# Normalising batch 1 of x from a transposed load, with the context work re-ordered around it

## The chip, the cores and the metric

The kernel runs on one core of one Trainium2 chip. The metric is the device time of one execution in microseconds (us). TensorE is called PE below, VectorE DVE, ScalarE ACT, GpSimd POOL and SyncE SP.

## What is computed

One decoder layer on x of shape (2, 512, 1024): self-attention with a head width of 256, a product of quantised activations with a quantised context, and a sparse feed-forward part, each on a layer norm of x and added to it. Cut to what matters here:

```python
def _L0_attn_ref(x, Wqkv, bqkv, Wo, bo):
    qkv = jnp.einsum('bsc,cf->bsf', x, Wqkv) + bqkv          # q, k, v: 256 wide each
    attn = jax.nn.softmax(jnp.einsum('bqd,bkd->bqk', q, k) * scale, axis=-1)
    out = jnp.einsum('bqk,bkd->bqd', attn, v)
    return jnp.einsum('bqd,dc->bqc', out, Wo) + bo

def _L0_xattn_ref(x1, x2, ...):                              # x2 is ctx_4096
    return jnp.matmul(fake_quant(x1, ...), fake_quant(x2, ...))

x = x + _L0_attn_ref(_layernorm(x), Wqkv, bqkv, Wo, bo)
x = x + _L0_xattn_ref(_layernorm(x), ctx_4096, ...)
x = x + _L0_ffn_ref(_layernorm(x), c1_w, c2_w, w1, w2t)
```

## The kernel before

x lies in SBUF as 8 tiles of 128 tokens by 1024 features; tiles 0 to 3 are batch 0, tiles 4 to 7 batch 1. PE needs the features on partitions. So each tile is normed by ACT (`norm`), transposed by PE in 8 blocks of 128x128 (`transpose_norm`, two jobs "T1" of four blocks for a tile), and cut into a high part (`hi_T` on ACT) and a low part (`lo_T` on DVE). Every product in the attention is then three matmuls, high by high, high by low, low by high (`split_mm`). The weights are cut in the same way, the high part on ACT and the low part on POOL.

All five engines run an order written out by hand, and wait on counting semaphores. PE writes its results into a ring of six PSUM banks. `job_order` lists the jobs in PE's order, and `take_bank` makes a job wait until the job six places ahead of it has been read out, which the counter `bank_free` says. DVE frees the banks, in its own program order, so a bank that DVE frees late holds up a PE job even when the data would be there.

The jobs of the first 110 us are: "T1" (transposes of normed x), "V" (values, 48 matmuls of 256 columns each), "Q" with c = 0 to 3 (queries and keys, 24 matmuls of 512 columns each), "S" (scores, four jobs of 6), "PT" (transposes of the softmax, four jobs of 4 blocks), "O" (values mixed by the softmax, two jobs of 12), "WO" (output projection, 6 each). The first number of a job is its batch.

Beside this, sixteen context tiles of 128x1024 are quantised. SP loads tile i into one of four slots (`ctx_slot`; slots 0 and 1 show as `ctx_raw` in the trace, slots 2 and 3 as `xn`), and the load of tile i waits until tile i-4 has left its slot (`q2_done`). ACT scales it (`scale_ctx`), DVE clips and rounds it (`round_ctx`), and POOL casts it to bf16 into `q2` (line 530). POOL also adds up the eight tiles of a batch (`add_q2`, line 515), adds the output bias to x (line 504) and cuts the low part of Wo (`cut_Wo`, line 521), which the first "WO" job waits for. Tiles 8 to 15 go to the place of the q and k weights, so tile 8 waits for job Q(1,3). Wo is loaded by ACT's queue at line 889, behind `hi_V(1, 1)`, into a place that the low part of x held.

The feed-forward part, from about 185 us to the end, is loops in which PE is never idle for long.

Of the kernel before, what the change touches and what calls it, by code (L numbers as in the profile page):

```python
# [98 lines left out]
def decoder_layer(nc, x_in, ctx_in, wqkv, bqk, bv, wo, bo, s1, z1, s2, z2, c1, c2, w1, w2, out):  # L99
# [35 lines left out]

    W_hi = at("W_hi", 96, [P, 3, KD, HD], F32R)
# [91 lines left out]
    with ExitStack() as ctx:  # L228
# [16 lines left out]
        W_loaded = [[sem(f"W_loaded{i}_{h}") for h in range(2)] for i in range(3)]  # L245
        bias_loaded = sem("bias_loaded")
# [28 lines left out]
        normed = sem("normed")  # L275
        vbias_added = sem("vbias_added")
# [127 lines left out]
        def _(sp):  # L404
# [81 lines left out]
        def _(pool):  # L486
# [15 lines left out]
            for t in range(NT):  # L502
                pool.wait_ge(normed, t + 1)
                nc.gpsimd.tensor_tensor(x[:, t, :], x[:, t, :], bo_b[:, :], ALU.add).then_inc(bo_added, 1)
# [32 lines left out]
            cut_Wo()  # L537
# [134 lines left out]
        def _(act):  # L672
# [40 lines left out]

            def hi_W(i, h):
# [4 lines left out]
            def hi_Q(b, c):  # L719
# [3 lines left out]
                if b == 1 and c == 0:  # L723
                    act.wait_ge(W_lo_done, 6)
# [134 lines left out]

            roots(0, 4)  # L860
            norm(0, 4)
            norm(0, 5)
            hi_Q(0, 0)
            hi_Q(0, 1)
            both(hi_T, 0, 4)
            norm(0, 6)
            hi_Q(0, 2)
            both(hi_T, 0, 5)
            norm(0, 7)
            hi_Q(0, 3)  # L870
            both(hi_T, 0, 6)
            both(hi_T, 0, 7)
# [3 lines left out]
            act.wait_ge(qp_ready, 1)  # L876
            for i in range(4):
                scale_ctx(i)
# [137 lines left out]
        def _(dve):  # L1016
# [56 lines left out]

            def lo_Q(b, c):
# [234 lines left out]
            lo_Q(0, 0)  # L1309
            lo_Q(0, 1)  # L1310
            lo_T(0, 4)
            lo_Q(0, 2)
            lo_T(0, 5)
            lo_Q(0, 3)
            lo_T(0, 6)
            lo_T(0, 7)

# [8 lines left out]
            nc.vector.scalar_tensor_tensor(rb_add, rb_mul, float(D), d1, ALU.mult, ALU.mult).then_inc(qp_ready, 1)  # L1326
            maxima(0)
# [4 lines left out]
            for i in range(4):  # L1332
                round_ctx(i)
# [139 lines left out]
        def _(pe):  # L1473
# [19 lines left out]
            def transpose_norm(rnd, t):  # L1493
# [4 lines left out]
                for h in range(2):  # L1498
# [6 lines left out]
                    last.then_inc(mm_done, 1)  # L1505

# [278 lines left out]
            project_qk(0, 0)  # L1785
            project_qk(0, 1)
            transpose_norm(0, 4)
            project_qk(0, 2)
            transpose_norm(0, 5)
            project_qk(0, 3)  # L1790
            transpose_norm(0, 6)
            transpose_norm(0, 7)
            for i in range(TB):
                scores(0, i)
            made("T1", NT - 1, 1)
            for c in range(4):
                project_qk(1, c)
            project_v(1, 0)
# [104 lines left out]
```

## Time and profile before

| | us |
|---|---|
| three executions | 793.71, 793.86, 794.48 |
| median | 793.86 |
| the profiled execution | 794.16 |
| its span in the trace | 792.3 |

The trace is of one execution. Its span is 1.9 us shorter than its own time, and its own time is 0.3 us over the median. PE's granted clock is full (1.00, which is 2.4 GHz) in every stretch of the trace.

### The profile page before, as it was taken

The page shows a single profiled execution, that of the slowest core. Times are in us where ns is not written, and L with a number is a line of the kernel's source. Part 1 is how long each engine was busy: PE and PEld are TensorE (multiplying, and loading weights), DVE is VectorE, ACT ScalarE, POOL GpSimd, SP SyncE. Part 2 cuts the span into 40 slices and gives each one's busy share as a digit, 9 for nine tenths or more (in the row PEclk, how much of TensorE's full clock was granted, in tenths as well). Part 3 has the DMA queues.
Part 4 walks back from the last instruction along what each step waited for, and adds up shares of the span by engine and source line. Part 5 has one row for each costly group of instructions (what it writes and reads, how often), then busy time and mean ns, then how long its engine had stood idle before and what let it go on. Part 6 is the DMA issues. An engine that isn't in the chain of part 4 may idle for free.

```text
span 792.3 us, 11474 instructions
## 1 busy us (share of the span) xinstructions
PE 785.7 (99%) x3883; PEld 641.2 (81%) x3888; DVE 590.7 (75%) x962; ACT 249.7 (32%) x375; POOL 433.2 (55%) x265
## 2 busy tenths in 40 slices
PE   8999999999999999999999999999999999999998
PEld 8888987478888888888888888888888888888886
DVE  6655669887884878887877778787878787777864
ACT  6457666973321130312121221303031212212030
POOL 3935898576999954545445252535454543525240
PEclk9999999999999999999999999999999999999999
DMA  9126402000111110111111111111111121111104
GB/s 340 66 106 212 164 19 89 8 1 8 60 54 60 37 49 29 54 60 53 60 53 60 53 60 53 58 34 37 43 53 60 53 60 53 60 53 53 53 18 195
DMA packets 22615, 53.22 MB, mean 67 GB/s; under 512 B 4544, under 2 KB 6592, under 8 KB 22464
## 3 DMA queue, kind: packets, MB, share of 16 engines
q1 hardware_dynamic: 22448, 51.86, 18.9%
q10 hardware_dynamic: 144, 1.05, 0.4%
q8 instruction: 15, 0.25, 0.1%
q14 instruction: 8, 0.07, 0.0%
HBM read 48.70 MB, written 4.19 MB: 67 GB/s over the span
## 4 chain that ended last, share of the span: by engine, by line
PE 96%; DVE 2%; DMA 1%; issue 0%; ACT 0%; SPq 0%; DVEq 0%
PE bank L1770 13%; PE bank L1771 13%; PE bank L1772 13%; PE bank L1675 12%; PE bank L1677 11%; PE bank L1676 11%; PE bank L1488 4%; PE bank L1490 4%; PE bank L1489 4%; PE bank L1629 3%; PE bank L1684 2%; PE bank L1666 2%; DMA x<-x_in 1%; PE bank L1645 1%; PE bank L1504 1%; DVE xT_lo L1070 1%
## 5 line engine op out<-in xcount | busy, mean ns | idle before, releaser
L1770 PE MATMUL bank<-w_hi,h_hi 128*128 128x512 f32 x448 | 176.2, 393 | 0.0
L1771 PE MATMUL bank<-w_lo,h_hi 128*128 128x512 f32 x448 | 175.0, 391 | 0.0
L1772 PE MATMUL bank<-w_hi,h_lo 128*128 128x512 f32 x448 | 174.4, 389 | 0.0
L1277 DVE TENSOR_TENSOR x<-bank,x 128x512 f32<-128x512 f32 x208 | 133.5, 685 | 50.0 <-PE bank L1772 50.0
L564 POOL TENSOR_TENSOR lo_r<-r,slot 128x512 fp32r<-128x512 f32 x52 | 67.5, 1299 | 155.9 <-ACT slot L787 155.9
L1772 PEld LDWEIGHTS bank<-w_hi,h_lo 128*128 128x128 f32 x448 | 84.1, 188 | 18.0
L1770 PEld LDWEIGHTS bank<-w_hi,h_hi 128*128 128x128 f32 x448 | 84.1, 188 | 15.7
L1771 PEld LDWEIGHTS bank<-w_lo,h_hi 128*128 128x128 f32 x448 | 84.4, 188 | 15.2
L1675 PE MATMUL bank<-xT_hi,slot 128*128 128x512 f32 x240 | 95.0, 396 | 0.0
L1676 PE MATMUL bank<-xT_lo,slot 128*128 128x512 f32 x240 | 93.5, 390 | 0.0
L1677 PE MATMUL bank<-xT_hi,lo_r 128*128 128x512 f32 x192 | 74.8, 390 | 0.0
L569 POOL TENSOR_TENSOR w_lo<-w_raw,w_hi 128x1024 fp32r<-128x1024 f32 x28 | 69.4, 2479 | 9.3 <-ACT w_hi L803 9.3
L830 ACT ACTIVATE h_hi<-bank 128x512 fp32r<-128x512 f32 x56 | 33.3, 599 | 127.3 <-DVE bank L1222 103.6
L649 POOL TENSOR_TENSOR tmp<-r,r 128x512 f32<-128x512 f32 x12 | 15.5, 1291 | 102.1 <-DMA r<-w 102.1
L787 ACT ACTIVATE slot<-r 128x512 fp32r<-128x512 f32 x66 | 41.3, 629 | 77.9 <-DMA r<-w 44.1
L814 ACT ACTIVATE sums<-bank 128x512 f32<-128x512 f32 x12 | 7.2, 598 | 171.5 <-PE bank L1677 171.5
L1218 DVE SCALAR_TENSOR_TENSOR h_lo<-bank,h_hi 128x512 fp32r<-128x512 f32 x56 | 38.4, 691 | 26.8 <-ACT h_hi L830 26.2
L1675 PE MATMUL bank<-T_hi,slot 128*128 128x512 f32 x144 | 57.3, 398 | 0.0
L1676 PE MATMUL bank<-T_lo,slot 128*128 128x512 f32 x144 | 56.0, 389 | 0.0
L1222 DVE TENSOR_TENSOR bank<-bank,sums 128x512 f32<-128x512 f32 x48 | 33.6, 700 | 26.7 <-PE bank L1684 25.8
L1676 PEld LDWEIGHTS bank<-xT_lo,slot 128*128 128x128 f32 x240 | 45.1, 188 | 8.8
L1675 PEld LDWEIGHTS bank<-xT_hi,slot 128*128 128x128 f32 x240 | 45.1, 188 | 8.8
(205 smaller groups left out, 1599.5 us busy)
## 6 DMA issues: line engine op xcount, KB each, us to landing
r<-w SPq DMA_DIRECT2D x56, 256.0 KB, 3.5
w_raw<-w SPq DMA_DIRECT2D x28, 512.0 KB, 4.0
x<-x_in SPq DMA_DIRECT2D x8, 512.0 KB, 10.0
ctx_raw<-ctx_in SPq DMA_DIRECT2D x8, 512.0 KB, 3.5
xn<-ctx_in SPq DMA_DIRECT2D x8, 512.0 KB, 4.8
out<-x SPq DMA_DIRECT2D x7, 512.0 KB, 2.7
W_raw<-wqkv SPq DMA_DIRECT2D x6, 512.0 KB, 10.5
c_raw<-c SPq DMA_DIRECT2D x112, 16.0 KB, 2.0
```

What stands on the lines that cost most here:

```text
L564: nc.gpsimd.tensor_tensor(lo[:, :, :], raw[:, :, :], hi[:, :, :].bitcast(F32), ALU.subtract).then_inc(A_lo_done, 1)
L569: nc.gpsimd.tensor_tensor(w2_lo[:, j, :], w2_raw[:, j, :], w2_hi[:, j, :].bitcast(F32), ALU.subtract).then_inc(w2_lo_done, 1)
L787: nc.scalar.activation(slot[:, :, :], src[:, :, :], ACT.Copy).then_inc(A_hi_done, 1)
L1218: nc.vector.scalar_tensor_tensor(h_lo[:, r, s], bank[c_bank(g, r, b)][:, :], 0.0, h_hi[:, r, s].bitcast(F32), ALU.max, ALU.subtract).then_ ...
L1222: return nc.vector.tensor_tensor(dst, bank[src][:, :], part, ALU.add).then_inc(sum_done, 1)
L1277: nc.vector.tensor_tensor(x[:, t, c], bank[unit_banks(g)[p]][:, :], x[:, t, c], ALU.add).then_inc(unit_added, 1)
L1675: nc.tensor.matmul(dst, hi[:, k, :], B_hi[:, k, :], start=first and k == 0, stop=False)
L1676: nc.tensor.matmul(dst, hi[:, k, :], B_lo[:, k, :], start=False, stop=False)
L1677: last = nc.tensor.matmul(dst, lo[:, k, :], B_hi[:, k, :], start=False, stop=closed and k == H - 1)
L1770: nc.tensor.matmul(dst, h_hi[:, j, m], w2_hi[:, j, c], start=j == 0, stop=False)
L1771: nc.tensor.matmul(dst, h_hi[:, j, m], w2_lo[:, j, c], start=False, stop=False)
L1772: last = nc.tensor.matmul(dst, h_lo[:, j, m], w2_hi[:, j, c], start=False, stop=j == GJ - 1)
```

## The change

The host passes a second copy of batch 1 of x with the features on partitions (`xT_in`). SP loads it in one DMA of 2 MB behind the last tile of x, into `xT_raw`, which lies where the low part of transposed batch 1 goes.

Batch 1 is then normed there. PE spreads the row scales and shifts of a pair of tiles over all partitions, by four 128x128 transposes of a broadcast column (`spread_rows`, job "R"). DVE multiplies and adds in place (`norm_xT`, two halves of 128x1024 each, a multiply and an add for each), ACT takes the high part (`hi_xT`), POOL the low part (`lo_xT`, in the place of `lo_T` on DVE). The transposes of tiles 4 to 7, the four ACT norms and the eight `hi_T` and `lo_T` of these tiles are gone. The bias additions of tiles 4 to 7 no longer wait for the norm.

The job V(1,0) moves ahead of the scores of batch 0. Context loads start behind Q(0,3). Context tiles 0 to 3 are scaled and rounded ahead of the softmax of batch 0, around V(1,0). Tiles 13, 14 and 15 each move one place back on ACT and DVE; tile 15's rounding now stands behind the maxima of batch 1 and ahead of `inverse_sums(1)`. On POOL the low part of Wo is cut ahead of tile 15 in place of behind the sum `add_q2(0, 5)`, and two sums no longer wait for the rounding of tile 8.

The core of the diff (a mechanical change of line numbers and of the counter for `normed` is left out):

```diff
-    jobs = both("T1", 0) + both("T1", 1) + both("T1", 2) + [("V", 0, 0)] + both("T1", 3) + [("V", 0, 1)]
-    jobs += [("Q", 0, 0), ("Q", 0, 1)] + both("T1", 4) + [("Q", 0, 2)] + both("T1", 5)
-    jobs += [("Q", 0, 3)] + both("T1", 6) + both("T1", 7)
+    jobs = both("T1", 0) + both("T1", 1) + both("T1", 2) + [("V", 0, 0)] + both("T1", 3)
+    jobs += [("V", 0, 1), ("Q", 0, 0), ("R", 0), ("Q", 0, 1), ("R", 1), ("Q", 0, 2), ("Q", 0, 3), ("V", 1, 0)]
     jobs += [("S", 0, i) for i in range(4)]
-    jobs += [("Q", 1, c) for c in range(4)] + both("V", 1)
+    jobs += [("Q", 1, c) for c in range(4)] + [("V", 1, 1)]
...
+            sp.dma_start(xT_raw[:, :, :], xT_in).then_inc(xT_loaded, 16)
-            sp.wait_ge(mm_done, nth("T1", 7, 1) + 1)
+            sp.wait_ge(mm_done, nth("Q", 0, 3) + 1)
...
+            def lo_xT(p):
+                for h in range(2):
+                    pool.wait_ge(xT_hi_done, 2 * p + h + 1)
+                    at_pair = token_pair(p, h)
+                    nc.gpsimd.tensor_tensor(xT_lo[1][at_pair], xT_raw[at_pair], xT_hi[1][at_pair].bitcast(F32),
+                                            ALU.subtract).then_inc(xT_lo_done, 1)
+            add_bo(0, 1, 2, 3)
+            lo_xT(0)
+            add_bo(4)
+            lo_xT(1)
+            add_bo(5, 6, 7)
...
+            def hi_xT(p):
+                for h in range(2):
+                    if h == 0:
+                        act.wait_ge(xT_normed, p + 1)
+                    else:
+                        act.wait_ge(bank_free, nth("R", p) + 1)
+                    at_pair = token_pair(p, h)
+                    nc.scalar.activation(xT_hi[1][at_pair], xT_raw[at_pair], ACT.Copy).then_inc(xT_hi_done, 1)
...
+            def norm_xT(p):
+                dve.wait_ge(mm_done, nth("R", p) + 1)
+                dve.wait_ge(xT_loaded, 16)
+                row = job_bank("R", p)[:, :].rearrange("p (s o m) -> p s o m", s=2, o=1)
+                scale, shift = (row[:, s].to_broadcast([P, 4, 2 * P]) for s in range(2))
+                for h in range(2):
+                    part = xT_raw[token_pair(p, h)]
+                    link(nc.vector.tensor_tensor(part, part, scale, ALU.mult))
+                    last = nc.vector.tensor_tensor(part, part, shift, ALU.add)
+                    if h == 0:
+                        last.then_inc(xT_normed, 1)
+                free(last)
...
+            def spread_rows(p):
+                pe.wait_ge(rstd_ready, nth_chain(0, TB) + 1)
+                take_bank("R", p)
+                for s, rows in enumerate((rstd, nmr)):
+                    for i in range(2):
+                        t, c = TB + 2 * p + i, (2 * s + i) * P
+                        last = nc.tensor.transpose(job_bank("R", p)[:, c:c + P],
+                                                   rows[:, t:t + 1].to_broadcast([P, P]), id_f[:, :])
+                last.then_inc(mm_done, 1)
```

On PE, around the job Q(0,2). `bank` is the PSUM ring, `id_f` the identity, and the matmuls of `xT` and `W` are those of the projection. Before:

```order
L1490 MATMUL bank<-xT_hi_50,W_lo 128x512
L1504 MATMUL bank<-id_f,xn 128x128 [waits bank_free,normed]
L1504 MATMUL bank<-id_f,xn 128x128 x3
L1504 MATMUL bank<-id_f,xn 128x128 [waits bank_free]
L1504 MATMUL bank<-id_f,xn 128x128 x3
L1488 MATMUL bank<-xT_hi_50,W_hi 128x512 [waits W_lo_done,bank_free]
```

And now, behind Q(0,0), where `rstd` and `nmr` are the scales and shifts:

```order
L1534 MATMUL bank<-xT_hi_50,W_lo 128x512
L1558 MATMUL bank<-id_f,rstd 128x128 [waits bank_free,rstd_ready]
L1558 MATMUL bank<-id_f,rstd 128x128
L1558 MATMUL bank<-id_f,nmr 128x128 x2
L1532 MATMUL bank<-xT_hi_50,W_hi 128x512 [waits W_lo_done,bank_free]
```

Eight transposes for each of four tiles have become four for each of two pairs, and they stand one projection earlier.

On POOL, from context tile 8 (`q_1`) to the end of the sums of batch 0 (`q_sum`). Before:

```order
L530 TENSOR_SCALAR q_1_73<-ctx_raw 128x1024 [waits mm_done]
L530 TENSOR_SCALAR q_1_73<-ctx_raw 128x1024 [waits ctx_rounded]
L530 TENSOR_SCALAR q_1_73<-xn 128x1024 [waits ctx_rounded] x2
L515 TENSOR_TENSOR q_sum_83<-q_sum_83,q_0_72 128x1024 [waits summing]
L530 TENSOR_SCALAR q_1_73<-ctx_raw 128x1024 [waits ctx_rounded] x2
L515 TENSOR_TENSOR q_sum_83<-q_sum_83,q_0_72 128x1024 [waits summing]
L530 TENSOR_SCALAR q_1_73<-xn 128x1024 [waits ctx_rounded] x2
L515 TENSOR_TENSOR q_sum_83<-q_sum_83,q_0_72 128x1024 [waits summing]
L521 TENSOR_TENSOR Wo_lo<-Wo_raw,Wo_hi 128x2048 [waits Wo_hi_done]
L515 TENSOR_TENSOR q_sum_83<-q_sum_83,q_0_72 128x1024 [waits summing] x2
```

Now:

```order
L558 TENSOR_SCALAR q_1_74<-ctx_raw 128x1024 [waits ctx_rounded,mm_done]
L558 TENSOR_SCALAR q_1_74<-ctx_raw 128x1024 [waits ctx_rounded]
L558 TENSOR_SCALAR q_1_74<-xn 128x1024 [waits ctx_rounded] x2
L541 TENSOR_TENSOR q_sum_84<-q_sum_84,q_0_73 128x1024 [waits summing]
L558 TENSOR_SCALAR q_1_74<-ctx_raw 128x1024 [waits ctx_rounded] x2
L541 TENSOR_TENSOR q_sum_84<-q_sum_84,q_0_73 128x1024 [waits summing]
L558 TENSOR_SCALAR q_1_74<-xn 128x1024 [waits ctx_rounded]
L547 TENSOR_TENSOR Wo_lo<-Wo_raw,Wo_hi 128x2048 [waits Wo_hi_done]
L558 TENSOR_SCALAR q_1_74<-xn 128x1024 [waits ctx_rounded]
L541 TENSOR_TENSOR q_sum_84<-q_sum_84,q_0_73 128x1024 [waits summing] x3
```

The cut of Wo has moved ahead of the cast of tile 15 and of one sum.

On DVE, from the rounding of tile 12 to the maxima of batch 1 there are, now:

```order
L1187 TENSOR_SCALAR ctx_raw<-ctx_raw 128x1024 [waits ctx_scaled]
L1138 TENSOR_TENSOR bank<-bank,bv_b 128x512 [waits mm_done]
L1142 TENSOR_TENSOR v_lo_69<-bank,v_hi_67 128x512 [waits hi_done]
L1162 TENSOR_TENSOR pT_lo<-bank,pT_hi 128x4x128 [waits hi_done] x2
L1187 TENSOR_SCALAR ctx_raw<-ctx_raw 128x1024 [waits ctx_scaled]
L1162 TENSOR_TENSOR pT_lo<-bank,pT_hi 128x4x128 [waits hi_done] x2
L1187 TENSOR_SCALAR xn<-xn 128x1024 [waits ctx_scaled]
L1392 TENSOR_SCALAR ones_r<-id_f 128x128
```

and behind the maxima, where before the reciprocals (`pinv`, which free the banks of the scores) came at once:

```order
L1150 TENSOR_SCALAR nbias<-smax 128x1 [waits vec]
L1187 TENSOR_SCALAR xn<-xn 128x1024 [waits ctx_scaled]
L1157 RECIPROCAL pinv<-psum_row 128x1 [waits exp_done] x4
L1168 TENSOR_TENSOR oT_lo_79<-bank,oT_hi_77 128x512 [waits hi_done] x2
L1162 TENSOR_TENSOR pT_lo<-bank,pT_hi 128x4x128 [waits hi_done] x4
```

The rounding of tile 15 (`xn<-xn`) now stands between the maxima and the reciprocals.

## Rows read from the trace of the kernel before

**Rows 1.** Page: busy time by engine; then who PE waited for, longest first.
```profile
PE 785.7 (99%) x3883; PEld 641.2 (81%) x3888; DVE 590.7 (75%) x962; ACT 249.7 (32%) x375; POOL 433.2 (55%) x265
PE bank L1645 <- DVE xT_lo L1070: 0.6, 1, 0.6
```

**Rows 2.** Timeline of PE: start us, us, engine, line, op, out<-in, count.
```profile
32.33 0.39 PE L1488 MATMUL bank<-xT_hi,W_hi 128*128 128x512 f32 x1
...
37.77 1.03 PE L1504 MATMUL bank<-id_f,xn 128*128 128x128 f32 x8
38.56 0.48 PE L1488 MATMUL bank<-xT_hi,W_hi 128*128 128x512 f32 x1
38.88 0.40 PE L1489 MATMUL bank<-xT_lo,W_hi 128*128 128x512 f32 x1
39.11 0.39 PE L1490 MATMUL bank<-xT_hi,W_lo 128*128 128x512 f32 x1
...
50.47 1.91 PE L1504 MATMUL bank<-id_f,xn 128*128 128x128 f32 x16
52.29 0.47 PE L1488 MATMUL bank<-k_hi,q_hi 128*128 128x512 f32 x1
```

**Rows 3.** Timeline of DVE: the last step of the norm statistics, and two low parts.
```profile
32.18 0.13 DVE L1062 SCALAR_TENSOR_TENSOR nmr<-mv,bank 128x4 f32<-128x4 f32 x1
...
39.36 1.28 DVE L1070 TENSOR_TENSOR xT_lo<-bank,xT_hi 128x512 fp32r<-128x512 f32 x2
```

**Rows 4.** Timeline of PE, later: V(1,0), PT(0), PT(1) and WO(0,0) start.
```profile
79.59 0.28 PE L1488 MATMUL bank<-W_hi,xT_hi 128*128 128x256 f32 x1
...
91.11 1.91 PE L1576 MATMUL bank<-id_f,probs 128*128 128x128 f32 x16
...
103.77 1.91 PE L1576 MATMUL bank<-id_f,probs 128*128 128x128 f32 x16
...
105.43 0.49 PE L1488 MATMUL bank<-Wo_hi,oT_hi 128*128 128x512 f32 x1
```

**Rows 5.** Timelines of DVE and POOL: two roundings and the POOL work beside them.
```profile
62.03 1.24 DVE L1142 TENSOR_SCALAR ctx_raw<-ctx_raw 128x1024 f32<-128x1024 f32 x1 [0.44 <-ACT ctx_raw L763]
77.34 2.35 DVE L1142 TENSOR_SCALAR ctx_raw<-ctx_raw 128x1024 f32<-128x1024 f32 x1 [0.44 <-ACT ctx_raw L763]
...
61.69 1.04 POOL L530 TENSOR_SCALAR q<-ctx_raw 128x1024 bf16<-128x1024 f32 x1 [12.12 <-DVE ctx_raw L1142]
...
76.99 2.15 POOL L515 TENSOR_TENSOR q_sum<-q 128x1024 fp32r<-128x1024 bf16 x1 [1.36 <-DVE ctx_raw L1142]
```

**Rows 6.** View of the tile `ctx_raw` from 83.0 to 84.5 us: tile 12's load.
```profile
DMA to landing us min/median/max: 3.5/3.5/3.5
```

**Rows 7.** Timeline of ACT: tile 12, high part of V(1,1), Wo, softmax transposes.
```profile
86.79 1.25 ACT L763 ACTIVATE ctx_raw<-ctx_raw,qp,qd 128x1024 f32<-128x1024 f32 x1
...
92.04 0.60 ACT L736 ACTIVATE v_hi<-bank 128x512 fp32r<-128x512 f32 x1 [1.57 <-DVE bank L1093]
...
92.54 1.08 ACT L752 ACTIVATE pT_hi<-bank 128x512 fp32r<-128x512 f32 x2
...
96.86 1.93 ACT L897 ACTIVATE Wo_hi<-Wo_raw 128x2048 fp32r<-128x2048 f32 x1
```

**Rows 8.** Timeline of DVE: V(1,1), tile 15, two maxima of batch 1.
```profile
91.31 0.70 DVE L1093 TENSOR_TENSOR bank<-bank,bv_b 128x512 f32<-128x512 f32 x1
...
96.88 0.69 DVE L1142 TENSOR_SCALAR xn<-xn 128x1024 f32<-128x1024 f32 x1 [0.21 <-ACT xn L763]
...
97.62 0.69 DVE L1104 TENSOR_REDUCE smax<-bank 128x1 f32<-128x512 f32 x1
...
98.41 0.68 DVE L1104 TENSOR_REDUCE smax<-bank 128x1 f32<-128x512 f32 x1
```

**Rows 9.** Timeline of POOL: the cut of Wo, and the first corrections of x.
```profile
100.77 4.60 POOL L521 TENSOR_TENSOR Wo_lo<-Wo_raw,Wo_hi 128x2048 fp32r<-128x2048 f32 x1
...
131.72 10.13 POOL L551 TENSOR_TENSOR x<-x,corr 128x1024 f32<-128x1024 f32 x4 [3.35 <-ACT xn L704]
```

More of the change, by code:

```diff
@@ L96, in nth_chain, with decoder_layer @@
     return next(n for n, (r, first, count) in enumerate(CHAINS) if r == rnd and first <= t < first + count)
-def decoder_layer(nc, x_in, ctx_in, wqkv, bqk, bv, wo, bo, s1, z1, s2, z2, c1, c2, w1, w2, out):
+def decoder_layer(nc, x_in, xT_in, ctx_in, wqkv, bqk, bv, wo, bo, s1, z1, s2, z2, c1, c2, w1, w2, out):
     D = x_in.shape[2]
@@ L275, in decoder_layer @@
         normed = sem("normed")
+        xT_normed = sem("xT_normed")
+        xT_hi_done = sem("xT_hi_done")
+        xT_lo_done = sem("xT_lo_done")
         vbias_added = sem("vbias_added")
@@ L501, in _, with add_bo @@
             pool.wait_ge(bias_loaded, 48)
-            for t in range(NT):
-                pool.wait_ge(normed, t + 1)
-                nc.gpsimd.tensor_tensor(x[:, t, :], x[:, t, :], bo_b[:, :], ALU.add).then_inc(bo_added, 1)
+            def add_bo(*tiles):
+                for t in tiles:
+                    if t < TB:
+                        pool.wait_ge(normed, t + 1)
+                    else:
+                        pool.wait_ge(mv_done, t + 1)
+                    nc.gpsimd.tensor_tensor(x[:, t, :], x[:, t, :], bo_b[:, :], ALU.add).then_inc(bo_added, 1)
+            def lo_xT(p):
[9 more added lines that the diff above has]
+            add_bo(5, 6, 7)
             def add_q2(b, i):
@@ L730, in hi_V @@
                 act.wait_ge(vbias_added, 2 * b + i + 1)
+                if (b, i) == (1, 0):
+                    act.wait_ge(W_lo_done, 6)
                 if (b, i) == (0, 0):
@@ L860, in _ @@
             roots(0, 4)
-            norm(0, 4)
-            norm(0, 5)
             hi_Q(0, 0)
             hi_Q(0, 1)
-            both(hi_T, 0, 4)
-            norm(0, 6)
+            hi_xT(0)
             hi_Q(0, 2)
-            both(hi_T, 0, 5)
-            norm(0, 7)
+            hi_xT(1)
             hi_Q(0, 3)
-            both(hi_T, 0, 6)
-            both(hi_T, 0, 7)
+            act.wait_ge(qp_ready, 1)
+            scale_ctx(0)
+            scale_ctx(1)
+            hi_V(1, 0)
+            scale_ctx(2)
+            scale_ctx(3)
             for i in range(TB):
                 exp(0, i)
-            act.wait_ge(qp_ready, 1)
-            for i in range(4):
-                scale_ctx(i)
             for c in range(4):
@@ L1309, in _ @@
             lo_Q(0, 0)
+            norm_xT(0)
             lo_Q(0, 1)
-            lo_T(0, 4)
+            norm_xT(1)
             lo_Q(0, 2)
[L1313 to L1316, printed above, removed]
             dve.wait_ge(qp_loaded, 64)
@@ L1326, in _ @@
             nc.vector.scalar_tensor_tensor(rb_add, rb_mul, float(D), d1, ALU.mult, ALU.mult).then_inc(qp_ready, 1)
+            lo_Q(0, 3)
+            round_ctx(0)
+            round_ctx(1)
+            lo_V(1, 0)
+            round_ctx(2)
+            round_ctx(3)
             maxima(0)
@@ L1330, in _ @@
             nc.vector.tensor_copy(id_b[:, :], id_f[:, :]).then_inc(id_b_ready, 1)
-            for i in range(4):
-                round_ctx(i)
             for c in range(4):
@@ L1785, in _ @@
             project_qk(0, 0)
+            spread_rows(0)
             project_qk(0, 1)
-            transpose_norm(0, 4)
+            spread_rows(1)
             project_qk(0, 2)
-            transpose_norm(0, 5)
             project_qk(0, 3)
-            transpose_norm(0, 6)
-            transpose_norm(0, 7)
+            pe.wait_ge(xT_lo_done, 2)
+            project_v(1, 0)
             for i in range(TB):
                 scores(0, i)
-            made("T1", NT - 1, 1)
+            pe.wait_ge(xT_lo_done, 4)
             for c in range(4):
                 project_qk(1, c)
-            project_v(1, 0)
             project_v(1, 1)
```

31 lines of the change are left out of this document (17 added, 14 removed).

## The prediction, as it was put on record

> **What bounds the kernel now.** I read the page first: PE is busy for 99% of the span, and the waits of PE add up to little (the longest behind the start is 0.6 us, on DVE at line 1645) [rows 1]. So PE's own work is the time, and a change pays only by what it takes off PE. Next I read PE's timeline where the transposes of batch 1 stand, to price them [rows 2], and then, since the change also turns the order on ACT, DVE and POOL, the stretch from 80 to 106 us on each of them [rows 4 to 9]. What the reader should see there: the cut of Wo on POOL ends at 105.37 [rows 9], and the first output projection, which needs it, starts at 105.43 [rows 4]. PE does not wait there now, but it has less than 0.1 us in hand. Anything that brings PE there earlier gains only if POOL and DVE come earlier too.
>
> **What PE loses and gets.** The transposes of tile 4 hold PE from 37.77 to 38.56, 0.79 us, and the first matmul behind them takes 0.32 us to the next where 0.23 is usual: 0.88 in all [rows 2]. Tile 5 is like it: 0.9. The 16 transposes of tiles 6 and 7 take 50.47 to 52.29, with the same 0.09 behind: 1.9. Together 3.7 us for 32 transposes. The change adds 8 such transposes in two pieces, at 0.11 each: 0.9 us. Net on PE: 2.8 us less.
>
> **The new wait at the first piece.** `spread_rows(0)` needs the shifts `nmr`, which end at 32.18 + 0.13 = 32.31 [rows 3]. PE comes there at 32.33 [rows 2]. With about 0.1 us from DVE to PE, that costs 0.1 us. Matmuls of Q(0,1) queue behind it.
>
> **The norm on DVE, ACT and POOL: hidden.** No row shows a 128x1024 operation with one operand in PSUM of this form. The nearest is the pair of 128x512 subtractions from a bank, 1.28 us [rows 3], so 1.2 us for each of four operations, 4.8 us for a pair of tiles; at double that it would be 9.6. DVE starts pair 0 behind `lo_Q(0, 0)` at about 34, and frees R(0) at 39. ACT's two copies end near 41 and POOL's two subtractions (2.4 us each, half of the cut of Wo [rows 9]) near 45. V(1,0) needs them at 49.7. So there is 4.7 us of cover, and it would hold even at 1.9 us for each operation. Pair 1 is needed only 11 us later, at the projections. What leaves these engines (four norms, eight copies, eight subtractions) is worth nothing, as they were hidden. The 2 MB load has to land by 34. It is the size of four loads like that of tile 12 (3.5 us each [rows 6]), so it takes up to 14 us behind the last tile of x, and it is issued behind all of x and W. I put it at nothing; rival 4 has the other end.
>
> **PE up to the softmax of batch 0.** On the clock of the trace, V(1,0) takes 5.76 us (half of 79.59 to 91.11 [rows 4]). It moves from behind Q(1,3) to ahead of the scores. So Q(1,3), which ended at 79.59, ends at 79.59 - 2.8 + 0.1 + 5.76 = 82.7. V(1,1) ends at 88.4, the four PT jobs at 90.1 (1.66 us [rows 4]).
>
> This is the step that matters. **Tiles 8 to 15 start on POOL only behind Q(1,3), now 3.1 us later, while all that waits for POOL is due 2.7 us earlier.**
>
> **POOL and DVE do not run these operations side by side.** A rounding on DVE takes 0.69 us by itself (96.88 [rows 8]). The one at 62.03 took 1.24 and ended at 63.27; POOL's cast beside it ended at 62.73. The one at 77.34 took 2.35 and ended at 79.69; POOL's sum beside it ended at 79.14 [rows 5]. Both end 0.55 us behind the end of POOL's instruction: the rounding waits for POOL and then runs. The subtractions from a bank (1.28 for two at 39.36 [rows 3]) ran beside POOL's bias additions at their usual length.
>
> The Trainium skill ("SBUF — State Buffer", "SBUF: two separate sides") says that DVE in a two-port mode and GpSimd share a port pair that is locked for a whole instruction, the later one blocking fully. By that rule, the trace agrees, a rounding behind the 4.6 us cut of Wo waits for all of it, and this speaks against putting them side by side, as the change does.
>
> **The chain behind Q(1,3), step by step.** Cast 1.04 [rows 5], sum 2.15 [rows 5], scale 1.24 [rows 7], about 0.2 from PE's last matmul to another engine (91.11 to 91.31 [rows 4, 8]) and 0.05 to 0.1 between other engines.
>
> - Casts of tiles 8 and 9: 82.9 to 85.0. ACT has scaled tile 10 by 84.75 (high part of Q(1,3) 0.6, scale 1.24), its rounding meets cast 9 and ends at 85.5; cast 10 ends at 86.6; the rounding of tile 11 meets it, ends at 87.2; cast 11 ends at 88.3. The sum `add_q2(0, 3)` follows, to 90.4.
> - Tile 12 loads when cast 8 is over, 83.9, and takes 3.5 us [rows 6]: scaled by 88.7, its rounding comes 0.4 to 0.5 us behind the start of that sum and ends at 91.0. DVE does the bias of V(1,1) only then, to 91.6 (now at once, at 91.31 for a job that ended at 91.11), ACT the high part to 92.2, DVE the low part to 92.9. The job S(1,1) stands six behind V(1,1), and PE comes there at 90.1 + 0.1 + 1.37 = 91.6. It gets the bank at 93.0. **First stall: 1.45 us.**
> - ACT: two softmax copies (1.0), scale of tile 13, 94.3. Rounding 95.0, cast 96.1, sum `add_q2(0, 4)` to 98.3. ACT has two more copies and tile 14 by 96.45; the rounding meets the sum and ends at 98.85. Cast 14 to 99.95, then the cut of Wo to 104.5 (4.6 us [rows 9]). The high part of Wo comes 4.8 us behind that of V(1,1) and takes 1.9 [rows 7], so it is over by 98.9 and does not hold the cut.
> - DVE: four maxima at 0.79 [rows 8] from 98.9, to 102.1. Then the rounding of tile 15 meets the cut of Wo and ends at 105.1. Behind it are the reciprocals that free the score banks. PE comes to PT(1,0), which needs the first of them, at 93.0 + 3 x 1.37 + 5.45 = 102.6, and starts at 105.3. **Second stall: 2.7 us.** PT(1) takes 1.66 and the first output projection starts at 106.95. The low part of Wo is there by then, and so are the two low parts of O, 1.3 us behind the reciprocals. The exponentials (tile 15 now stands ahead of them on ACT) end at about 103 and don't decide.
>
> Put through the same steps the kernel before gives 105.55 for that start, where the trace has 105.43. So the difference is 106.95 - 105.55 = 1.4 us later. By terms: -2.8 + 0.1 + 1.45 + 2.7 = +1.45.
>
> **Behind that point** PE has no wait up to 171 us, and the order is unchanged. POOL ends its sums some 2.8 us later than now, 1.4 later against PE; ahead of the corrections of x it is idle for 3.35 us, until ACT's norm [rows 9], and that takes it up. So 1.4 us stays to the end. The profiled execution of 794.16 would be 795.6; with the median at 793.86, 795.3.
>
> **Rivals.**
>
> 1. *The rounding of tile 12 comes ahead of the sum.* It takes a load of at most 3.0 us in place of 3.5, or POOL 0.5 us later. Then the bias of V(1,1) is done 1.5 us earlier, the first stall is gone and the chain behind ends 2.1 us earlier; the second stall stays, at about 2.0 (PE 2.7 us early, held to 103.2). -2.8 + 0.1 + 2.0 = -0.7: 793.1. For it: the margin is half a microsecond. Against: the load's own row says 3.5.
> 2. *The roundings don't wait for POOL where PE depends on them*, because DVE gets in first, or the long cut does not lock it out. Then the first output projection waits only for the cut of Wo, some 0.8 us: -2.7 + 0.8 = -1.9, and with a better course of POOL -2.7: 791.2 to 792.0. Against it speak both rows of the pair above.
> 3. *Slower by more.* The mechanism: behind the second stall PE's granted clock falls from 2.4 to 1.2 GHz. The trace shows full clock throughout, and the longest wait in it behind the start is 0.6 us [rows 1], so it can't say. If only the four PT jobs ran at half the clock, 1.66 would become 3.3: 1.7 us more, 797.0. It decides from the point where the two stalls pass 4.3 us in sum (over 0.2% slower then even without it); I have 4.15.
> 4. *The load of x transposed delays the first 25 us.* It would need to be served ahead of x or W; it is issued last. Price: up to the 14 us above. I give it 3 in 100, which are part of rival 3's share.
>
> In the Trainium skill ("TensorE: Matmul & The Clock Gate", "HAM oscillation — how this bites in real kernels") idle waits between bursts are said to bring the clock back down; no run here shows it. By that rule the time would be that of rival 3.
>
> **Chances and range.** What I forecast 60 in 100 (794.8 to 795.8, as the steps are good to a few tenths), rival 1 15, rival 2 11, rival 3 with 4 14. This kernel's measurement can tell some 0.2% from no change, 1.6 us. Faster by that (under 792.3): rival 2, 0.12. Slower by that (over 795.4): rivals 3 and 4 and a third of my case, 0.33. Within: 0.55. The range takes in my case, rival 1 and the near part of rival 3: 792.8 to 796.8.
>
> **What would show it.** In the new trace: PE without the 32 transposes and with 8 (right if PE reaches V(1,0) at about 49.7 without a wait); the rounding of tile 12 at about 88.8 with some 2.1 us; a wait of PE on `v_lo` ahead of S(1,1); the rounding of tile 15 at about 102 with 3 us, ending 0.55 behind the cut of Wo; PT(1) at 105.3. It is wrong if the roundings keep 0.7 us beside POOL, or if PE waits for `xT_lo` at V(1,0) or at Q(1,0).

## The result, and the profile after

The changed kernel takes 797.71 us (median of 6 runs, 797.41 to 798.09), the kernel before 793.98 (6 runs, 793.70 to 794.48). The ratio is 1.0046, 95% interval 1.0033 to 1.0059: slower by 3.7 us. The forecast was 795.3, and the result lies above the range, whose end was 796.8.

The profiled execution of the changed kernel, by its page: busy time by engine, and the granted clock in 40 slices. Beside [rows 1], PE's busy time is 0.6 us less, for 3.7 us more of span.

```profile
span 796.0 us, 11421 instructions
PE 785.1 (99%) x3859; PEld 639.4 (80%) x3864; DVE 611.7 (77%) x962; ACT 245.5 (31%) x367; POOL 442.0 (56%) x269
...
PEclk9999999999999999999999999999999999999999
```

Who PE waited for (total us, times, longest). The first and the third are new: before, the longest wait behind the start was 0.6 [rows 1].

```profile
PE bank L1631 <- DVE pinv L1157: 2.4, 1, 2.4
PE bank L1834 <- POOL id_f L498: 1.5, 1, 1.5
PE bank L1532 <- DVE v_lo L1142: 1.3, 1, 1.3
PE bank L1700 <- DVE xT_lo L1101: 0.6, 1, 0.6
...
PE bank L1671 <- ACT q1T L806: 0.2, 1, 0.2
```

PE's timeline (start us, us, engine, line, operation, idle before it and who ended it): the first piece of broadcast, R(0), in its two parts, then the starts of V(1,0), PT(0), S(1,1), PT(1) and WO(0,0). They answer to [rows 2, 4].

```profile
32.62 0.43 PE L1558 MATMUL bank<-id_f,rstd 128*128 128x128 f32 x2
32.89 0.38 PE L1558 MATMUL bank<-id_f,nmr 128*128 128x128 f32 x2
...
49.94 0.28 PE L1532 MATMUL bank<-W_hi,xT_hi 128*128 128x256 f32 x1
...
88.67 1.91 PE L1631 MATMUL bank<-id_f,probs 128*128 128x128 f32 x16
93.26 0.50 PE L1532 MATMUL bank<-k_hi,q_hi 128*128 128x512 f32 x1 [1.29 <-DVE v_lo L1142]
...
105.45 3.43 PE L1631 MATMUL bank<-id_f,probs 128*128 128x128 f32 x16 [2.37 <-DVE pinv L1157]
108.53 0.77 PE L1532 MATMUL bank<-Wo_hi,oT_hi 128*128 128x512 f32 x1
```

The 16 transposes of PT(1) hold PE for 108.53 - 105.45 = 3.08 us, where before they held it for 1.66. The windows of 1 us say why. Columns: stretch; its length; busy us and counts of PE, PE's weight loads, DVE, ACT, POOL; then the granted clock, the share of the DMA engines and GB/s.

```profile
104.00:105.00 1.00, 0.00 (x0) 0.00 (x0) 1.00 (x1) 0.18 (x1) 0.77 (x1) 1.00 0.00 0
105.00:106.00 1.00, 0.55 (x4) 0.56 (x5) 1.00 (x6) 0.00 (x0) 0.59 (x1) 0.88 0.00 0
106.00:107.00 1.00, 1.00 (x7) 1.00 (x6) 0.78 (x3) 0.60 (x1) 1.00 (x2) 0.50 0.00 0
107.00:108.00 1.00, 1.00 (x6) 1.00 (x5) 0.84 (x2) 0.60 (x1) 1.00 (x1) 0.50 0.00 0
108.00:109.00 1.00, 1.00 (x6) 1.00 (x5) 0.84 (x2) 0.69 (x2) 0.92 (x2) 0.50 0.07 16
109.00:110.00 1.00, 1.00 (x5) 0.78 (x5) 0.84 (x2) 0.98 (x2) 1.00 (x1) 0.92 0.00 0
```

Behind the wait of 2.37 us PE works at half the clock, 1.2 GHz, from about 105.8 to 109.2 us (windows of 0.2 us place the two ends). That is 3.4 us, in which 1.7 us of work at full clock get done. The page's 40 slices don't show it: a slice is 20 us long, and 3.4 us of it at half the clock round away.

Timelines of DVE and of POOL around the two waits: the roundings of tiles 12 and 15, and what POOL did beside them.

```profile
89.90 1.34 DVE L1187 TENSOR_SCALAR ctx_raw<-ctx_raw 128x1024 f32<-128x1024 f32 x1 [2.44 <-ACT ctx_raw L799]
91.16 0.68 DVE L1138 TENSOR_TENSOR bank<-bank,bv_b 128x512 f32<-128x512 f32 x1
...
102.31 3.02 DVE L1187 TENSOR_SCALAR xn<-xn 128x1024 f32<-128x1024 f32 x1
105.24 0.33 DVE L1157 RECIPROCAL pinv<-psum_row 128x1 f32<-128x1 f32 x4
```

```profile
88.55 2.14 POOL L541 TENSOR_TENSOR q_sum<-q_sum,q 128x1024 fp32r<-128x1024 f32 x1
...
100.20 4.57 POOL L547 TENSOR_TENSOR Wo_lo<-Wo_raw,Wo_hi 128x2048 fp32r<-128x2048 f32 x1
105.41 1.05 POOL L558 TENSOR_SCALAR q<-xn 128x1024 bf16<-128x1024 f32 x1 [0.64 <-DVE xn L1187]
```

The cut of Wo ends at 104.77, the rounding at 105.33, 0.56 us behind it; the rounding of tile 12 ends at 91.24, 0.55 behind the sum (90.69).

**Where the 3.7 us are**, by PE's start times in both traces: PT(0) at 88.67 instead of 91.11, so -2.44. From PT(0) to PT(1) 16.78 us instead of 12.66: +4.12, the two waits with PE's restarts. PT(1) +1.42 and the rest of the half clock +0.28, together 1.70. That leaves PE 3.38 later than before at the start of O(1,0) (114.38 against 111.00). The first matmul behind the last transposes of x, ahead of the feed-forward part, starts 3.76 later than before (175.47 against 171.71), so another 0.38 was lost in between. -2.44 + 4.12 + 1.70 + 0.38 = 3.76.

### The profile page after: what moved, and what is told of

Read it like the earlier page. It is cut to its first block, busy times and chain, and to the rows that moved or that the text cites. A ratio compares the mean times of both kernels' runs of the same rounds, so it can differ in the third digit from the quotient of the medians.

```text
span 796.0 us, 11421 instructions
## 1 busy us (share of the span) xinstructions
PE 785.1 (99%) x3859; PEld 639.4 (80%) x3864; DVE 611.7 (77%) x962; ACT 245.5 (31%) x367; POOL 442.0 (56%) x269
## 3 DMA queue, kind: packets, MB, share of 16 engines
q1 hardware_dynamic: 22592, 53.96, 19.6%
## 4 chain that ended last, share of the span: by engine, by line
PE 90%; DVE 4%; ACT 2%; DMA 2%; issue 1%; POOL 0%; SPq 0%; ACTq 0%; DVEq 0%
PE bank L1825 13%; PE bank L1826 13%; PE bank L1827 13%; PE bank L1730 12%; PE bank L1732 11%; PE bank L1731 11%; PE bank L1532 3%; PE bank L1534 3%; PE bank L1533 3%; PE bank L1684 2%; PE bank L1739 2%; PE bank L1721 2%; DMA x<-x_in 1%; PE bank L1700 1%; DVE xT_lo L1101 1%
## 6 DMA issues: line engine op xcount, KB each, us to landing
xT_raw<-xT_in SPq DMA_DIRECT2D x1, 2048.0 KB, 19.6
```

## The experiments

Twelve kernels ran, in four groups; each ratio is against runs of the kernel before on the same chip. The changed kernel itself was measured beside a median before of 793.98; the groups had 794.16 (e1 to e4), 793.99 (e5 to e8), 793.97 (e9, e10) and 794.40 (e11, e12). So a difference of medians between groups is good to some tenths of a us only. Kernels with the same code up to 32 us started R(0) anywhere between 31.8 and 33.0 us in their profiled executions. So single spans differ by up to 1.2 us from what lies ahead of any edit, and below I take stretches inside one trace, and medians.

**e1_fill: the same wait, filled.** The cheapest way to part the wait from the clock is to keep PE at work while it waits.

```
             scores ... both("O", 0)
+            for i in range(20):
+                transpose of the identity into the spare bank 7
             for i in range(TB): transpose_probs(1, i)
```

> The changed kernel, with 20 transposes of the identity into the idle bank 7 on PE ahead of PT(1,0), where PE otherwise waits from about 103.1 to 105.45 us. They write nothing that is read. Theory (the clock falls because PE idles for 2.4 us, and this costs another 1.7 us): PT(1) starts at 105.4 as before, the granted clock stays full, its 16 transposes take 1.66 us in place of 3.08, time 797.7 - 1.7 = 796.0. Rival (the slow stretch has another cause, such as the operations beside it): the 16 transposes still take 3.1 us, 797.7.

Measured: 796.17 us, ratio 1.0025 (1.0015 to 1.0035). PE's timeline and a window:

```profile
102.99 2.34 PE L1861 MATMUL bank<-id_f 128*128 128x128 f32 x20
105.53 1.64 PE L1631 MATMUL bank<-id_f,probs 128*128 128x128 f32 x13 [0.19 <-DVE pinv L1157]
```

```profile
106.00:107.00 1.00, 1.00 (x11) 1.00 (x10) 0.99 (x3) 0.78 (x2) 1.00 (x2) 1.00 0.00 0
```

The first view ends at 107 us; by the whole timeline the 16 transposes of PT(1) take 1.72 us and WO(0,0) starts at 107.25, where it was 108.53. PT(1) starts where it did, at 105.5, but the clock is full, with the same work on DVE and POOL beside it. Work that does nothing makes the kernel 1.5 us faster by the medians (1.7 by the ratios; 1.6 at the matmul at 175 us in the two traces). The clock is thus a cause of its own, worth 1.5 to 1.7 us.

**e2_round15, e3_round12, e4_both: each wait taken away, then both.** In e2 the rounding of tile 15 stands behind the low parts of O, so nothing that PE needs is queued behind it; in e3 the rounding of tile 12 stands behind the low part of V(1,1).

```
-            round_ctx(15)          # e2
             inverse_sums(1)
             lo_O(0, 0)
             lo_O(0, 1)
+            round_ctx(15)
...
-            round_ctx(12)          # e3
             lo_V(1, 1)
+            round_ctx(12)
```

> The changed kernel with the rounding of tile 15 on DVE behind the two low parts of O, in place of ahead of the reciprocals. Theory (the reciprocals queue behind a rounding that waits for POOL's cut of Wo): PE starts PT(1) at 102.9 without a wait, the clock stays full, the first output projection waits only for the cut of Wo (104.8) and starts at about 105.3 where it was 108.5: 797.7 - 3.2 = 794.5. Rival (PT(1) waits for the exponentials, which ACT does behind tile 15): PT(1) still starts at about 105, time within 0.5 of 797.7.

> The changed kernel with the rounding of tile 12 on DVE behind the two operations of V(1,1), in place of ahead of them. Theory: the wait ahead of S(1,1), 1.3 us, is gone; Wo and the cut of it come about 2 us earlier; PT(1) starts at 103.4 and still waits some 2 us behind the rounding of tile 15. The first output projection at 105.1 if the clock stays full, 106.6 if it falls: 794.3 or 795.8. Rival (the first wait comes from V(1,1)'s own work): no change, 797.7.

> Both moves of the runs e2_round15 and e3_round12 in the changed kernel. Theory: PE has neither wait, PT(1) starts at 101.4 and the first output projection at 103.2, 2.3 us ahead of the kernel before: 793.98 - 2.3 and some 0.4 that the changed kernel loses elsewhere, 792.1. Rival (a further engine holds PE as soon as these two waits are gone): 793.5 or more.

Measured: e2 794.48, ratio 1.0002 (0.9993 to 1.0012). e3 795.58, 1.0014 (1.0005 to 1.0024). e4 793.44, 0.9991 (0.9981 to 1.0000). The starts of PT(1) in e2 and e3:

```profile
102.27 1.91 PE L1631 MATMUL bank<-id_f,probs 128*128 128x128 f32 x16
```

```profile
103.13 2.66 PE L1631 MATMUL bank<-id_f,probs 128*128 128x128 f32 x16 [2.46 <-DVE pinv L1157]
```

e2 gives back 3.2 us of 3.7, as expected: the second wait and its clock are nearly the whole loss, and the reciprocals stood behind the rounding, not behind the exponentials. e3 takes away the first wait alone, PE comes earlier to the same rounding, and the second wait is 2.46. Its ten runs are in two groups: five at a mean clock of 0.997 to 0.998 of full took 795.7 to 796.5 us, five at 1.0 took 794.0 to 795.4. One kernel shows both outcomes, 1.3 us apart in their means. The profiled run is of the first group (clock 0.998): the clock is at half from 104.2 to 107.6 us.

e4 missed its forecast of 792.1 by 1.3. Its trace: WO(0,0) waited 1.00 us for the low part of O, behind exponentials that stood on ACT behind the scaling of tile 15, and that behind the high part of Wo:

```profile
96.35 1.92 ACT L927 ACTIVATE Wo_hi<-Wo_raw 128x2048 fp32r<-128x2048 f32 x1 [2.59 <-DMA Wo_raw<-wo]
98.17 1.23 ACT L799 ACTIVATE xn<-xn,qp,qd 128x1024 f32<-128x1024 f32 x1
99.31 0.67 ACT L783 ACTIVATE probs<-bank,nbias 128x512 f32<-128x512 f32 x1
```

Issued at 88.8, Wo took 7.5 us to land; issued at 91.9 in the changed kernel it took 4.8. I had carried 4.8 over.

**e6_split: does a rounding wait for one instruction of POOL, or until POOL is idle?**

```
-                tensor_tensor(Wo_lo[:, :, :], Wo_raw[:, :, :], Wo_hi[:, :, :], subtract)
+                tensor_tensor(Wo_lo[:, 0, :], Wo_raw[:, 0, :], Wo_hi[:, 0, :], subtract)
+                tensor_tensor(Wo_lo[:, 1, :], Wo_raw[:, 1, :], Wo_hi[:, 1, :], subtract)
```

> The changed kernel, with GpSimd's split of Wo written as two instructions of 128x1024 instead of one of 128x2048; the order on every engine is as it was. If VectorE's two-port rounding of tile 15 waits only for the GpSimd instruction that is running (they take turns at instruction ends), it gets in between the two halves, ends near 103 us instead of 105.3, PT(1,0) starts near 103.2 after a gap of some 0.5 us, the granted clock stays full, and the time is 794.2 (797.7 less 2.0 of wait and 1.5 of clock). Rival: the rounding waits until GpSimd is idle, through both halves, and the time stays at 797.7.

Measured: 793.97, ratio 1.0001 (0.9991 to 1.0010), forecast 794.2; 3.7 us come back, which is the time of the kernel before and no more. The rounding on DVE, and the two halves on POOL:

```profile
101.91 0.85 DVE L1188 TENSOR_SCALAR xn<-xn 128x1024 f32<-128x1024 f32 x1
```

```profile
99.81 2.40 POOL L547 TENSOR_TENSOR Wo_lo<-Wo_raw,Wo_hi 128x1024 fp32r<-128x1024 f32 x1
102.16 2.83 POOL L548 TENSOR_TENSOR Wo_lo<-Wo_raw,Wo_hi 128x1024 fp32r<-128x1024 f32 x1
```

The rounding gets in where the first half ends and takes 0.85 instead of 3.02 us; the second half pays for it, 2.83 instead of 2.40. PT(1) starts at 102.88 after 0.2 us. So the two engines change over at the ends of instructions. Same order, same work, one instruction in two pieces: that is the smallest mend, and it keeps the order of the change. The first wait is still there, 1.28 us ahead of S(1,1), and eats about half of what the change takes off PE.

**e5_load_alone and e9_small_ops: the new load in the old order.** e5 keeps the transposed load and the two pieces of broadcast, and puts V(1,0), the context tiles, the sums and the cut of Wo back. e9 then moves eight small operations.

```
             lo_Q(0, 2)
+            lo_Q(0, 3)                # e9
             scales of the quantisers (eight operations of 128x1)
-            lo_Q(0, 3)
```

> Only batch 1 of x through the transposed load: features normed on partitions, the two broadcast jobs in place of the 32 transposes. The context tiles, V(1,0), the sums of q2 and the split of Wo stand in the order of the kernel before. If the two waits of the changed kernel (1.3 us ahead of S(1,1), 2.4 us ahead of PT(1,0)) and the clock of 1.2 GHz behind the second come from the moved order alone, this kernel has none of them and keeps what the transposes saved: WO(0,0) starts 0.9 us earlier than before (2.8 us less PE work on transposes, 0.1 us wait, and the wait for Wo's split that then stands ahead of WO(0,0)), time 793.1 to 793.5 beside 794.2 of the kernel before. Rival: the load or the norming on partitions costs time itself; then it is at 794.2 or above, with waits of PE between 27 and 50 us, and the moved order would be less guilty than I say.

> e5_load_alone with VectorE's eight small operations on the quantiser's scales (128x1) put behind the low part of Q(0,3) instead of ahead of it. In e5_load_alone three of them took 1.45, 2.19 and 2.20 us beside GpSimd's work, the low part of Q(0,3) ended at 52.4 us, TensorE had waited 3.0 us ahead of S(0,0), and the granted clock went to half from 53.8 to 57 us. If those operations and the missing cover of V(1,0) are the cause, the low part follows its high part at once (ends 51.0), the wait is 1.5 us, the clock stays full, and the time is 793.4 beside the 796.3 of e5_load_alone. Rival: the transposed load or the norming costs the time in another place; then it stays above 795.

Measured: e5 796.31, ratio 1.0037 (1.0020 to 1.0054); e9 797.11, ratio 1.0038 (1.0025 to 1.0052). Both forecasts missed. e5: PE's wait ahead of the first score, DVE beside it, and two windows:

```profile
52.57 0.47 PE L1527 MATMUL bank<-k_hi,q_hi 128*128 128x512 f32 x1 [3.02 <-DVE k_lo L1119]
```

```profile
47.28 2.19 DVE L1362 TENSOR_TENSOR qd<-qd 128x1 f32<-128x1 f32 x1
...
49.57 2.20 DVE L1364 SCALAR_TENSOR_TENSOR qd<-qd 128x1 f32<-128x1 f32 x1
51.69 0.74 DVE L1119 SCALAR_TENSOR_TENSOR k_lo<-bank,bqk_s,k_hi 128x512 fp32r<-128x512 f32 x1
```

```profile
54.00:55.00 1.00, 1.00 (x4) 0.81 (x3) 0.37 (x1) 0.00 (x0) 1.00 (x2) 0.50 1.03 414
55.00:56.00 1.00, 1.00 (x4) 0.81 (x3) 0.48 (x2) 0.45 (x1) 1.00 (x1) 0.50 0.98 401
```

Operations on one number for each partition take 2.2 us, because they read two operands from SBUF and stand beside POOL's 128x1024 instructions. The rows around them bear this out: the operations of the same size with one operand from SBUF took 0.14 beside POOL's instructions (47.04 and 47.11), a two-operand one at 49.39, just as POOL changed over at 49.41, took 0.14, and the two long ones ended within 0.1 us of POOL's instruction (49.47 and 49.41, 51.77 and 51.74). In the kernel before POOL was idle there, and all eight took 0.14 to 0.16. The changed kernel has the three long ones too (1.44, 2.19 and 2.25 us), and PE doesn't wait for them. Before the change 16 transposes stood between Q(0,3) and the scores [rows 2]; in the changed kernel V(1,0) does, 5.76 us of PE work. The transposes were thus cover, and moving V(1,0) forward is what replaced it. In e9 the wait shrank to 1.66 as forecast, the clock stayed full there, and PT(0) came 3.06 us earlier than in e5 (forecast 2.9, which is 796.3 - 793.4). But the small operations then ran against POOL until 58.8 us, and a wait of 2.0 us for the low part of V(1,1) came at 95.27, with the clock at half behind it:

```profile
97.00:98.00 1.00, 1.00 (x4) 0.79 (x3) 1.00 (x3) 1.00 (x3) 0.59 (x1) 0.50 1.01 426
98.00:99.00 1.00, 1.00 (x4) 0.81 (x3) 0.79 (x2) 0.99 (x2) 0.45 (x1) 0.50 0.03 8
```

The traces show what it is: DVE adds the bias of V(1,1) only behind the rounding of tile 13, whose scaling starts at 91.18 us, and in e5 at 91.28. So PE comes 3.06 us earlier, and the context tiles come when they did. The small operations have a part in this, as the maxima now begin behind them, at 58.71 (54.63 in e5), and the first context tile is scaled at 62.65 (61.55 in e5); how large a part is open. What e5 and e9 settle is that blaming the order alone and not the load was too simple: the load needs the new order around V(1,0), and an order that holds V(1,1) behind two roundings gives back what the load saves.

**e7_exps, e8_exps_wo: is there a version that beats both?** e7 is e4 with the scaling of tile 15 behind the exponentials and the copies of O; e8 also issues the load of Wo ahead of the high part of V(1,1), and puts q2(0,4)'s sum behind the cut of Wo.

```
             Wo_hi
-            scale_ctx(15)
             exp(1, 0..3), hi_O(0, 0), hi_O(0, 1)
+            scale_ctx(15)
```

> Both roundings moved back as in the kernel before this one (e4_both), and ScalarE's scaling of tile 15 put behind the exponentials of batch 1 and the copies of O. e4_both ended 1.3 us above its forecast; WO(0,0) waited 1.0 us for VectorE's low part of O, behind the exponentials, behind the scaling of tile 15 (1.2 us). If that chain held it, the exponentials start 1.1 us earlier, WO(0,0) starts at 103.0 instead of 103.98 (the split of Wo ends at 102.93 and is next), time 792.4. Rival: what is gained ahead of WO(0,0) is taken back behind 126 us, where VectorE and GpSimd stay where they were; then the time is that of e4_both, 793.4.

> As e7_exps, and the load of Wo is issued ahead of the high part of V(1,1) instead of behind it (0.8 us earlier), and GpSimd's sum q2(0,4) stands behind the split of Wo, not ahead of tile 14. If the chain load of Wo, its high part, its split bounds WO(0,0) in e7_exps, that job starts near 102.3, time 791.7. Rival: the load lands no earlier since it shares the queues with the context tiles, or the quantised stage behind 126 us absorbs the gain; then 792.4 or what e7_exps shows.

Measured: e7 792.99, ratio 0.9987 (0.9978 to 0.9997). e8 793.28, ratio 0.9990 (0.9981 to 1.0000). Forecast were 792.4 and 791.7. e7 is the best version measured: 1.0 us faster than the kernel before, of the 2.7 us that the change takes off PE. Inside the traces both do what was forecast: WO(0,0) starts at 103.06 and 102.21 (forecast 103.0 and 102.3). But in e8 a wait stands at 144 us, and DVE and POOL show its source:

```profile
144.21 0.61 PE L1669 MATMUL bank<-id_b,q 128*128 128x128 bf16 x8 [1.15 <-ACT q1T L805]
```

```profile
139.56 1.83 DVE L1191 TENSOR_SCALAR xn<-xn 128x1024 f32<-128x1024 f32 x1
```

```profile
131.00 9.83 POOL L577 TENSOR_TENSOR x<-x,corr 128x1024 f32<-128x1024 f32 x4
```

**e10_corr, e11_corr5, e12_corr5_late_wo: the same collision, 35 us later.** The rounding of q1 at 139.56 takes 1.83 us, ending 0.56 behind POOL's four corrections. If that is the cause, a correction held back until the rounding is done frees PE.

```
             for t in range(NT):
+                if t == 3: pool.wait_ge(q1_rounded, 5)     # e10: 3
                 add_corr(t)
```

> e8_exps_wo with one wait more on GpSimd: its correction of tile 3 waits until VectorE has rounded q1 of tile 2. In e8_exps_wo WO(0,0) started 1.8 us earlier than in e4_both, but the rounding took 1.83 us beside GpSimd's corrections (0.64 alone), ScalarE's copy of the transposed q1 came late, and TensorE waited 1.15 us at 144.2 us. If the shared port takes the gain back there, that wait is gone and the time is 1.1 us below the 793.3 of e8_exps_wo: 792.1. Rival: the late copy has another cause, or the late correction holds up VectorE's next use of it; then 793.3 or above.

> e10_corr waited for the third rounding of q1, which was long done when GpSimd came to tile 3, so it had no effect. Here GpSimd's correction of tile 3 waits for the fifth rounding (q1 of tile 4), the one that took 1.83 us beside the corrections in e8_exps_wo. If the shared port takes the gain back there, the rounding takes 0.7 us, TensorE's wait of 1.15 us at 144 us is gone, and the time is 1.1 us below the 793.3 of e8_exps_wo: 792.2. Rival: the late correction holds up what reads it, or another chain is next; then 793.3 or above.

> The same wait in e7_exps, whose load of Wo and sums stand as in the changed kernel. Its two waits for the copied q1 in the quantised stage are 0.38 and 0.42 us. If the same rounding is their cause, both go and the time is 792.3 instead of 793.0; if only the second, 792.6. Rival: 793.0 or above, when the waits come from ScalarE's own queue.

Measured: e10 793.43, ratio 0.9995 (0.9986 to 1.0004): its wait was met long before, so it is e8 a second time, with 1.17 us of wait where e8 had 1.15. e11 793.38, ratio 0.9990 (0.9981 to 0.9998). e12 794.24, ratio 0.9996 (0.9987 to 1.0005). Rows of e11, DVE, POOL and PE:

```profile
140.05 0.64 DVE L1193 TENSOR_SCALAR xn<-xn 128x1024 f32<-128x1024 f32 x1
...
142.04 1.64 DVE L1193 TENSOR_SCALAR xn<-xn 128x1024 f32<-128x1024 f32 x1
```

```profile
140.76 2.36 POOL L577 TENSOR_TENSOR x<-x,corr 128x1024 f32<-128x1024 f32 x1 [1.77 <-DVE xn L1193]
```

```profile
145.08 3.61 PE L1684 MATMUL bank<-q,q1T 128*128 128x512 bf16 x16 [0.96 <-DVE x L1212]
```

The rounding is back at 0.64 us and PE's wait for the copy is gone, so the cause was read rightly. But the held correction now meets the next rounding (1.64 us), and PE waits 0.96 us for what DVE does behind it. The collision moved, and the time did not. e12 had nothing to free: in e7 the fifth rounding (141.58) and the sixth (143.57) both took 0.64 already. Holding the correction back put it beside the sixth, which took 1.62, and gave PE the same wait of 0.96 where e7 has none, while the two waits for the copy stayed (0.23 and 0.41, in e7 0.38 and 0.42). They so don't come from that rounding. The forecast of 792.3 missed by 1.9, 0.4 of it the chip (the median before is 794.40). In the profiled runs the matmul at 171 us starts 1.52 later than in e7 (171.90 against 170.38): 0.73 is e12's later start (R(0) at 32.98 against 32.25), the rest the new wait less 0.16 of the old ones.

## Why the prediction was wrong, by its steps

**What held.** PE's own saving: PT(0) came 2.44 us early, as -2.8 + 0.1 and a start that was 0.25 later give (the first projection starts at 27.11, before at 26.86; I had nothing there, and the scatter of 1.2 us between equal starts covers it). The norm was hidden: V(1,0) starts at 49.94 without a wait, and DVE's four operations for each pair took 1.21 to 1.22 us each, priced at 1.2. The 2 MB load took 19.6 us from issue (11.4) to landing (31.0), more than the 14 that I had allowed, and still landed 3.2 us ahead of DVE's first use at 34.2. Both waits came where they were put, for the reason given. The first: 1.29 us, forecast 1.45; the second: 2.37, forecast 2.7; in start times, with PE's restarts, together 4.12, forecast 4.15. The rounding of tile 15 was to start at about 102 and take 3 us: 102.31 and 3.02. PT(1) was to start at 105.3: 105.45.

**What was off without effect.** The rounding of tile 12 began at 89.90, forecast 88.8, and ended at 91.24, forecast 91.0. It met the same sum of POOL, so its end is set by POOL's end and not by its own start. That is why an error of 1.1 us on a load became one of 0.2.

**The step that failed** is "PT(1) takes 1.66" behind the second stall, with "So 1.4 us stays to the end". It took 3.08, since the granted clock fell to half. I had the mechanism and nearly its price (rival 3: 3.3 us for PT(1), 797.0) but gave it, with rival 4, 14 in 100. The trace before has no wait over 0.6 us behind the start to test it by, and I had written that it can't say; yet the sum went by full clock as if it had. The bound that I gave for it, stalls of 4.3 us in sum, was a bound on the time and not on the clock: it fell with waits of 1.29 and 2.37. e1_fill shows the price alone, 1.5 to 1.7 us: 795.3 with it is 796.8 to 797.0, at the end of my range and beyond. The Trainium skill ("TensorE: Matmul & The Clock Gate", "HAM oscillation — how this bites in real kernels") said that idle waits between bursts bring the clock down, and here the trace agrees: 2.37 us of idle, then 1.2 GHz for 3.4 us. The waits in that section's example are 3 to 5 us long; here a shorter one did it, and the measurement decides.

**The rest**, a net 0.38 us between 120 and 175 us, with a wait of 0.25 for the copied q1 at 161.75, speaks against "PE has no wait up to 171 us". I had compared POOL's margin ahead of its corrections but not DVE's roundings beside them. In the changed kernel's trace the rounding of q1 at 144.13 takes 1.84 us and the one at 152.35 takes 2.77, beside POOL's corrections; the same two took 0.64 (142.91) and 0.69 (149.64) before. Behind the second, ACT waits 1.70 us for it ahead of the copies that PE needs. In e6, with the same order in this stage and PE there some 4 us earlier, they take 0.64 and 0.69, and PE has no such wait. So the late arrival brings the two engines together here as well; no run changed this alone. With this, 1.70 of clock + 0.38 + 0.25 at the start are 2.3 of the 2.4 us between 795.3 and 797.7.

**Rivals 1, 2 and 4.** The first wait did not go (rival 1). The roundings did wait for POOL, for each instruction singly, which e6 settled (rival 2). The load delayed nothing that a wait shows (rival 4): the first piece of broadcast starts 0.3 us later than PE came there before, of which 0.25 is the later start; whether the load has a part in that start, the scatter of 1.2 us hides.

## What to carry to other kernels

Price a wait of the engine that bounds the kernel with what follows it: if the trace before has no wait of that length, the clock behind it is unknown, and its price belongs in the forecast at even chances, not as a remote rival. Put no DVE rounding that something waits for beside a long POOL instruction: move it behind what is waited for, or cut POOL's instruction in two (e6, 3.7 us for one line). Before transposes or other small PE jobs are removed, look at which chain on the other engines they covered: with the old order (e5) the removed 2.8 us of PE work laid bare a wait of 3.0 us and then the clock, and the kernel became 2.3 us slower. And a saving on the engine that bounds the kernel is worth only what the other engines can follow: of 2.7 us the best version kept 1.0 (e7).

## What the runs showed of the hardware

- The clock. By the profiled executions, waits of PE of 0.96, 1.15, 1.29 and 1.66 us (e11, e8, the changed kernel, e9) left it at 2.4 GHz, and so did one of 1.82 us at 10.1 us (e1, ahead of the first transposes of x). Waits of 2.00 (e9), 2.37 (the changed kernel), 2.46 (e3) and 3.02 us (e5) were each followed by 3.4 us at 1.2 GHz, which began 0.3 to 1.2 us behind PE's restart. It is not the same in every run: five of e3's ten, one of e9's five and one of e5's seven stayed at full clock in the mean, and one of e11's eleven did not (0.997); their waits are not recorded. PE was busy without a gap ahead of each of them, in e8 and e11 with bf16 matmuls, in the others with fp32.
- POOL and DVE. A DVE rounding of 128x1024 (one SBUF source), or an operation with two SBUF sources, even one of 128x1, waits for the POOL instruction under way: 0.16 us becomes 2.2 (e5). Operations of 128x1 with one SBUF source did not (0.14 beside POOL, e5), nor did 128x1024 operations with one operand in PSUM (1.21 to 1.22 beside POOL). The rounding ended 0.55 to 0.56 us behind POOL's end at both stalls (90.69 and 91.24, 104.77 and 105.33), in e6, e8 and e11. In e6 it came in between two POOL instructions, and the one behind was 0.43 us longer.
- A load of 1 MB took 4.8, 6.8, 7.1, 7.5 and 7.6 us (the changed kernel, e8, e7, e4, e10). It was issued at 91.9 us in the first and at 88.1 to 89.2, beside more of the context loads, in the others; e8 and e10 have the same code there and differ by 0.8.
